# Row-maximum scores as two 512-column matmuls in a fused window-attention and linear-attention kernel

## The reference

```python
# layer 0: per window of S=64 tokens, C=128 channels, 8 heads of dh=16
normed = layernorm(win, ln1_g, ln1_b)
q, k, v = split(normed @ in_w.T + in_b)
scores = einsum('bhsd,bhtd->bhst', q, k) / sqrt(16)
attn = softmax(scores)
win = win + einsum('bhst,bhtd->bhsd', attn, v) @ out_w.T + out_b
h = layernorm(y, ln2_g, ln2_b)
y = y + silu(h @ fc1_w.T + fc1_b) @ fc2_w.T + fc2_b
# layer 1: per image, N = 1024 positions, E = 64
q, k, v = wq x + bq, wk x + bk, wv x + bv
out = wo ((q k^T / N) v) + bo + x
```

## Time and profile before

| | us |
|---|---|
| median of 3 runs (377.37 to 381.28) | 377.72 |
| profiled execution, its own time | 377.23 |
| its span, first to last instruction | 375.4 |
| PE busy in it | 349.0 (93%) |
| DVE busy | 294.3 (78%) |
| ACT busy | 241.7 (64%) |
| scores for the maxima, PE L611, 512 matmuls | 54.4 |

### The profile page before, as it was taken

One profiled execution on the slowest core, in us unless ns is written; L12 is line 12 of the kernel. 1 busy time (PEld: TensorE's weight loads), 2 busy tenths in 40 slices (PEclk: granted clock), 3 DMA queues, 4 the chain that ended last, 5 costly groups with the idle time before them and its releaser, 6 DMA issues.

```text
span 375.4 us, 9822 instructions
## 1 busy us (share of the span) xinstructions
PE 349.0 (93%) x3349; PEld 294.9 (79%) x3349; DVE 294.3 (78%) x863; ACT 241.7 (64%) x438; POOL 167.2 (45%) x176
## 2 busy tenths in 40 slices
PE   3679999999999999999999999999999999999764
PEld 2567788888888888888888888888888888878552
DVE  8387889798788878898788878898798878687452
ACT  1426677774969478784969478684969478664540
POOL 6353054644455434645455434635455434431420
PEclk9999999999999999999999999999999999999898
DMA  4133140403122121403122121403122120300101
GB/s 126 34 88 81 33 109 9 113 2 82 60 77 63 41 70 56 111 1 77 63 76 64 38 74 56 109 3 77 63 72 68 35 77 31 86 2 18 40 1 56
DMA packets 31570, 21.94 MB, mean 58 GB/s; under 512 B 22272, under 2 KB 23360, under 8 KB 31552
## 3 DMA queue, kind: packets, MB, share of 16 engines
q1 hardware_dynamic: 31552, 21.71, 21.1%
HBM read 4.92 MB, written 4.19 MB: 24 GB/s over the span
## 4 chain that ended last, share of the span: by engine, by line
PE 76%; DVE 6%; issue 4%; ACT 2%; POOL 1%; DVEq 0%; POOLq 0%; ACTq 0%
PE p_scoreT L634 12%; PE p_c L529 11%; PE p_score L611 9%; PE p_attn L649 9%; PE p_a L529 6%; PE p_scoreT L629 4%; PE p_a L593 4%; PE p_c L707 3%; PE p_d L529 3%; DVE xn_tok L1105 3%; PE p_c L678 2%; PE p_d L719 2%; PE p_a L577 2%; PE p_a L567 2%; PE p_c L684 2%
## 5 line engine op out<-in xcount | busy, mean ns | idle before, releaser
L910 ACT ACTIVATE probs<-p_scoreT 128x512 f32<-128x512 f32 x64 | 38.6, 603 | 35.1 <-PE p_scoreT L634 34.6
L465 POOL TENSOR_TENSOR hid_l<-hid,hid_h 128x512 fp32r<-128x512 f32 x30 | 40.3, 1364 | 43.5 <-ACT hid_h L944 41.6
L611 PE MATMUL p_score<-kd_h,qd_h 128*128 128x128 f32 (+1 forms) x512 | 54.4, 249 | 0.9 <-DVE row_max L1158 0.8
L611 PEld LDWEIGHTS p_score<-kd_h,qd_h 128*128 128x128 f32 (+1 forms) x512 | 50.0, 163 | 5.9 <-DVE row_max L1158 2.4
L649 PEld LDWEIGHTS p_attn<-vd,probs 128*64 128x64 f32 x1024 | 36.2, 139 | 22.2 <-issue 15.1
L470 POOL TENSOR_TENSOR y_l<-y,y_h 128x512 fp32r<-128x512 f32 (+1 forms) x17 | 20.5, 1208 | 69.4 <-ACT y_h L924 69.4
L1158 DVE TENSOR_REDUCE row_max<-p_score 128x8 f32<-128x512 f32 x64 | 43.9, 687 | 6.7 <-PE p_score L611 6.7
L649 PE MATMUL p_attn<-vd,probs 128*64 128x34 f32 x1024 | 45.7, 245 | 2.7 <-ACT probs L910 2.7
L457 POOL TENSOR_SCALAR kd_l<-k_l,head_a 128x512 fp32r<-128x512 f32 x16 | 26.7, 1669 | 33.5 <-DVE k_l L1140 19.8
L634 PE MATMUL p_scoreT<-qd_h,kd_h 128*128 128x256 f32 x128 | 41.3, 322 | 0.0
L449 POOL TENSOR_TENSOR rstd<-rstd,minus_half 128x4 f32<-128x4 f32 (+1 forms) x33 | 35.5, 1076 | 2.8
(11 more groups left out here) (183 smaller groups left out, 877.9 us busy)
## 6 DMA issues: line engine op xcount, KB each, us to landing
x_in<-in_x SPq DMA_DIRECT2D x16, 256.0 KB, 2.9
qd_h<-q_h SPq DMA_DIRECT2D x64, 64.0 KB, 2.0
qd_l<-q_l SPq DMA_DIRECT2D x64, 64.0 KB, 2.0
vd<-v_tok SPq DMA_DIRECT2D x64, 64.0 KB, 2.2
out<-out_sb SPq DMA_DIRECT2D x16, 256.0 KB, 2.1
fc_rows<-in_L_conv_fc_w SPq DMA_DIRECT2D x2, 128.0 KB, 2.5
in_w_rows<-in_L_conv_in_w SPq DMA_DIRECT2D x1, 192.0 KB, 2.7
out_w_rows<-in_L_conv_out_w SPq DMA_DIRECT2D x1, 64.0 KB, 2.4
```

The lines of the kernel that those rows point to most:

```text
L465: pool.tensor_tensor(hid_l[:, t], hid[:, t], hid_h[:, t].bitcast(F32), ALU.subtract).then_inc(hid_low[t], 1)
L611: last = pe.matmul(p_score[0:rows, 2 * KEYS * j:2 * KEYS * (j + 1)], qd_h[:, h.par, j, 2 * KEYS * p:2 * KEYS * p + rows], kd_h[:, h.par, 2 ...
L910: act.activation(probs[:, p % 2], p_scoreT[:].rearrange("row (win j q) -> row win j q", win=2, j=QUADS), ACT.Exp, scale=SCORE_SCALE).then_ ...
```

## The change

It has two parts.

1. **Scores for the maxima.** Now the keys are spread instead of q: a new tile `km_h`, zero outside its blocks, holds for each head pair j the keys of all windows in that pair's 32 rows only. The weights are `q_h` of the pair's 128 (64) queries, the moving operand is `km_h[:, par, :, window]`, four blocks of 128 columns: one matmul of 512 columns per window, two per pair of windows. `km_h` is filled from `kd_h` by four DMAs of 128 KB (`spread_k`), once both `kd_h` blocks are there. `q_h` has two parities now. The first score of a step waits for `km_dma`; the wait for `qd_h` and `kd_h` goes to `b_scoreT`. GpSimd zeroes both parities of `km_h` (4096 elements per partition each) in the prologue, and sets `vd` later.
2. **Order.** On TensorE `a_q` goes ahead of the tail's `c_fc2`, and `a_k` takes the place behind `c_yT`. On ScalarE `a_xn` goes behind `c_o` at the end of the step before, `a_q`, `a_k` and the first `a_k_block` ahead of `b_exp(1)`, the second right behind it. On VectorE `a_xn` goes ahead of `c_y1`, `a_q` ahead of `c_y2`, `a_k` ahead of `c_kv`.

```diff
-        q_h = sb("q_h", [C, HALF], F32R)
+        q_h = sb("q_h", [C, 2, HALF], F32R)
+        km_h = sb("km_h", [C, 2, QUADS, 2 * HALF], F32R)
...
+            def spread_k(h):
+
+                sp.wait_ge(kd_high[0], h.n())
+                sp.wait_ge(kd_high[1], h.n())
+                if h.follows(2):
+                    sp.wait_ge(score_ready[PAIRS - 1], h.n(2))
+                for j in range(QUADS):
+                    head_pair = slice(32 * j, 32 * j + 32)
+                    sp.dma_start(km_h[head_pair, h.par, j, :].bitcast(F32),
+                                 kd_h[head_pair, h.par].rearrange("p win a k -> p (win a k)").bitcast(F32)
+                                 ).then_inc(km_dma, 16)
...
             def prologue(loop):
                 sp.wait_ge(q_zero_set[0], 2)
                 spread_q(loop.half(0))
+                sp.wait_ge(km_zero_set[0], 1)
+                spread_k(loop.half(0))
                 sp.wait_ge(v_const_set, 5)
                 spread_v(loop.half(0))
...
                 rstd1_of(loop.half(0))
+                set_values()
                 pool.memset(qd_h[:, 1].bitcast(F32), 0.0).then_inc(q_zero_set[1], 1)
                 pool.memset(qd_l[:, 1].bitcast(F32), 0.0).then_inc(q_zero_set[1], 1)
+                pool.memset(km_h[:, 1].bitcast(F32), 0.0).then_inc(km_zero_set[1], 1)
                 k_low_block(loop.half(0))
...
             def b_score(h, p):
 
                 if p == 0:
-                    pe.wait_ge(q_high_dma, h.n(times=16 * QUADS))
-                    pe.wait_ge(kd_high[0], h.n())
-                    pe.wait_ge(kd_high[1], h.n())
+                    pe.wait_ge(q_high, h.n())
+                    pe.wait_ge(km_dma, h.n(times=16 * QUADS))
...
-                for j in range(QUADS):
-
-                    for win, rows in ((1, 2 * KEYS), (0, KEYS)):
-                        last = pe.matmul(p_score[0:rows, 2 * KEYS * j:2 * KEYS * (j + 1)],
-                                         qd_h[:, h.par, j, 2 * KEYS * p:2 * KEYS * p + rows],
-                                         kd_h[:, h.par, 2 * p + win], start=True, stop=True)
+                for win, rows in ((1, 2 * KEYS), (0, KEYS)):
+                    window = 2 * p + win
+                    last = pe.matmul(p_score[0:rows, :], q_h[:, h.par, 2 * KEYS * p:2 * KEYS * p + rows],
+                                     km_h[:, h.par, :, 2 * KEYS * window:2 * KEYS * (window + 1)], start=True, stop=True)
...
                 b_score(b, 2)
+                if with_a:
+                    a_q(a)
                 if with_tail:
                     c_fc2(tail)
                 b_attn(b, 0)
                 if with_c:
                     c_yT(c)
                 if with_a:
-                    a_q(a)
+                    a_k(a)
                 if with_tail:
                     c_kv(tail)
                 b_scoreT(b, 1)
                 b_score(b, 3)
                 if with_d:
                     d_kvT(loop, -1)
-                if with_a:
-                    a_k(a)
                 b_attn(b, 1)
```

More of the change, by code:

```diff
@@ L352, in spread_q @@
                     head_pair = slice(32 * j, 32 * j + 32)
-                    sp.dma_start(qd_h[head_pair, h.par, j, :].bitcast(F32), q_h[head_pair, :].bitcast(F32)
+                    sp.dma_start(qd_h[head_pair, h.par, j, :].bitcast(F32), q_h[head_pair, h.par, :].bitcast(F32)
                                  ).then_inc(q_high_dma, 16)
@@ L389, in step_even @@
                 spread_q(loop.half(1))
+                spread_k(loop.half(1))
                 spread_v(loop.half(1))
@@ L395, in step_odd @@
                     spread_q(loop.half(2))
+                    spread_k(loop.half(2))
                     spread_v(loop.half(2))
@@ L416, in _, with set_values @@
             pool.memset(minus_half[:], -0.5).then_inc(const_ready, 1)
-            pool.memset(vd[:], 0.0).then_inc(v_const_set, 1)
-            pool.wait_ge(v_const_set, 1)
-            for a in range(2):
-                for s in range(2):
-                    pool.memset(vd[64 * a:64 * a + 64, s, :, a, DH, :], 1.0).then_inc(v_const_set, 1)
-            pool.wait_ge(v_const_set, 5)
+            pool.memset(km_h[:, 0].bitcast(F32), 0.0).then_inc(km_zero_set[0], 1)
+            def set_values():
+                pool.memset(vd[:], 0.0).then_inc(v_const_set, 1)
+                pool.wait_ge(v_const_set, 1)
+                for a in range(2):
+                    for s in range(2):
+                        pool.memset(vd[64 * a:64 * a + 64, s, :, a, DH, :], 1.0).then_inc(v_const_set, 1)
+                pool.wait_ge(v_const_set, 5)
             def waited():
@@ L619, in b_scoreT @@
                 if p == 0:
+                    pe.wait_ge(q_high_dma, h.n(times=16 * QUADS))
                     pe.wait_ge(q_low_dma, h.n(times=16 * QUADS))
+                    pe.wait_ge(kd_high[0], h.n())
+                    pe.wait_ge(kd_high[1], h.n())
                     pe.wait_ge(kd_low[0], h.n())
@@ L876, in a_q @@
                 act.wait_ge(q_ready, h.n())
-                if h.follows(1):
-                    act.wait_ge(q_high_dma, h.n(1, times=16 * QUADS))
-                act.activation(q_h[:], p_a[0][:], ACT.Identity, bias=qkv_b[:, 0:1]).then_inc(q_high, 1)
+                if h.follows(2):
+                    act.wait_ge(q_high_dma, h.n(2, times=16 * QUADS))
+                if h.follows(2):
+                    act.wait_ge(score_ready[PAIRS - 1], h.n(2))
+                act.activation(q_h[:, h.par], p_a[0][:], ACT.Identity, bias=qkv_b[:, 0:1]).then_inc(q_high, 1)
             def a_k(h):
@@ L892, in a_k_block @@
                     act.wait_ge(scoreT_ready[PAIRS - 1], h.n(2))
+                if h.follows(2):
+                    act.wait_ge(km_dma, h.n(2, times=16 * QUADS))
                 act.wait_ge(k_high, h.n())
@@ L970, in prologue @@
                 a_v(a)
+                a_xn(loop.half(1))
             def step(loop, b, with_a, with_next, with_c, with_tail, with_d, with_last=False):
@@ L981, in step @@
                 if with_a:
-                    a_q(a)
+                    a_k(a)
+                    a_k_block(a, 0)
                 b_exp(b, 1)
                 if with_a:
-                    a_k(a)
-                    a_k_block(a, 0)
+                    a_k_block(a, 1)
                     a_v(a)
@@ L1003, in step @@
                     c_o(b)
+                if with_next:
+                    a_xn(next_a)
                 if with_d and not with_last:
@@ L1130, in a_q @@
                     dve.wait_ge(q_low_dma, h.n(1, times=16 * QUADS))
-                dve.scalar_tensor_tensor(q_l[:], p_a[0][:], qkv_b[:, 0:1], q_h[:].bitcast(F32),
+                dve.scalar_tensor_tensor(q_l[:], p_a[0][:], qkv_b[:, 0:1], q_h[:, h.par].bitcast(F32),
                                          ALU.add, ALU.subtract).then_inc(q_low, 1)
@@ L1293, in step @@
                 b_widen(b, 1)
+                if with_a:
+                    a_xn(a)
                 if with_c:
```

15 lines of the change are left out of this document (6 added, 9 removed).

## The result

| | before | after |
|---|---|---|
| median of 4 runs each, us | 377.55 (377.09 to 381.28) | 386.64 (385.47 to 389.18) |
| profiled execution, its own time, us | 377.23 | 389.18 |
| its span, us | 375.4 | 387.3 |
| TensorE busy, us | 349.0 (93%) | 346.0 (89%) |
| first score of step 0, us | 20.50 | 24.89 |

The account below looks back on a forecast made before the run. TensorE looked bound, but the new order would make VectorE bound the first half of a step. Terms 4.1 + 0.5 - 0.2 + 7 x 0.1 + 6 x 0.4 - 0.4 = +7.1 us on 377.23: 384.3, median 384.5, range 373.5 to 390.

Parts of the forecast that it names:

- first score: Prologue: the first score waits for the keys' DMAs, starting at 24.6 instead of 20.50; +4.1 us (3.8 to 4.7).
- step 0: First step: the second keys' DMAs land 17.6 us behind the first score, the step lasting 16.6; +0.5 us.
- step 1: Second step, with no tail and few pieces on VectorE; -0.2 us.
- seven even steps: Steps 2 to 14: the scores' savings vanish as TensorE waits for `xn_l` before q; +0.1 us each.
- six odd steps: Odd steps: `q_l` and `k_l` delay `kv_tok` on VectorE, so `d_kvT` starts 1.4 us later; +0.4 us each.
- step 15 and the rest: Last step, which has no stage a; -0.4 us.
- the 0.5 to 0.8 given as the sign: Before q in each step: TensorE would wait 0.5 to 0.8 us on `xn_l`.
- TensorE stays the bound: Rival: VectorE keeps up, so each of 14 steps saves 0.8 us; 370.2 us, chance 0.13.
- Half of it survives: Rival: waits in front of q shorten later ones, so 14 steps save 0.4 us each; 375.8 us, chance 0.2.
- Worse: Rival: no wait shortens another, even steps +0.3 us, odd +0.8; 388 us, chance 0.15.
- The keys are late in every step: Rival: SyncE's groups or landings take 2 us more, even steps +1 us; 391 us, chance 0.02.
- the signs given: Included even steps of 18.9 to 19.1 us, odd ones of 23.6 to 24.1, and the clock at full speed.

Follow-up runs that it names:

- experiment 1: Changed kernel plus 19 unread matmuls of 512 columns on TensorE, filling the wait before the first scores; 386.49 us, ratio 1.018 to the kernel before.
- experiment 3: Changed kernel's new order, but old scores in all steps and no spreading of keys; 383.41 us, ratio 1.011 to the kernel before.
- experiment 8: Changed kernel with the edits of experiment 2 and experiment 7, `c_kv` behind the fourth scores, q behind attention 0 where no tail; 376.25 us, ratio 0.993.
- experiment 9: As experiment 8, but `c_kv` moved behind the fourth scores in even steps alone; 371.54 us, ratio 0.982 to the kernel before.
- experiment 7: Changed kernel with the moves of experiment 5 (TensorE) and experiment 6 (VectorE) together; 379.36 us, ratio 1.002 to the kernel before.
- experiment 6: Changed kernel with two moves on VectorE: `y2` ahead of `q_l`, `kv_tok` ahead of `k_l`; 385.64 us, ratio 1.019 to the kernel before.
- experiment 4: Changed kernel's new scores, but the old order on TensorE, ScalarE and VectorE; 400.44 us, ratio 1.057 to the kernel before.
- experiment 5: Changed kernel with one move on TensorE: q behind the tail's `c_fc2`; 392.88 us, ratio 1.036 to the kernel before.
- experiment 2: Changed kernel, but step 0 takes the old scores and its keys are spread behind v; 381.45 us, ratio 1.007 to the kernel before.
- experiment 10: Order of experiment 9 with old scores in all steps and no key DMAs; 377.24 us, ratio 0.998 to the kernel before.

## Why the prediction came out right, and where it did not

The sign held, and so did the waits that were named. Most of the loss lies elsewhere than in the order, though: 9.3 of the 11.9 us are the first score and step 0, where the prediction had 4.6 of 7.1. The terms, against the profiled execution:

| term | predicted | measured | difference |
|---|---|---|---|
| first score | +4.1 | +4.39 | +0.3 |
| step 0 | +0.5 | +4.87 | **+4.4** |
| step 1 | -0.2 | +0.05 | +0.2 |
| seven even steps | +0.7 | +2.42 | +1.7 |
| six odd steps | +2.4 | +0.37 | -2.0 |
| step 15 and the rest | -0.4 | -0.15 | +0.2 |
| sum | +7.1 | +11.9 | +4.8 |

**The first score.** Read rightly from the earlier trace rows: the keys were issued from 20.56 (20.43 predicted) and landed in 2.4 us (2.3 taken). GpSimd's new memsets ended at 17.37 and `kd_l` was begun 0.17 later, at the same time as before: nothing, by little, as said.

**Step 0 is the term that was mis-sized, +0.5 for +4.87.** The prediction asked only whether the second set of keys would be late at its end, and took the clock to stay full. The 4.6 us of idle TensorE at the start, which it had itself worked out, were followed by a fall of the granted clock, and step 0 ran at half speed for most of its length: experiment 1 puts that at 2.1 to 3.0 us of the profiled step. The rest is open between the remaining clock loss and the order: q goes forward to a place where `xn_l` is not ready, and waits 1.33 us, and experiment 3, with no keys at all, has 18.70 for step 0, some of it clock.

The reason given for +0.5 was nevertheless a sound one. It reckoned 17.6 us from the first score to the landing of the second keys. In after's slowed step they kept nobody waiting. At the full clock they do: they land 17.8 us behind the first score in experiments 8 and 9, and end step 0 there. The half microsecond by which q's DMAs are earlier is 0.2 to 0.4 (8.0 us behind the first score in experiment 1 and 8.2 in experiment 3, against 8.4).

**Even steps: VectorE does bound the first half, and one cover was missed.** `xn_l` was ready at 4.77 and q started at 4.92 (5.02 predicted for both), and `c_fc2` ended at 7.2 as predicted. TensorE's wait before q was 0.41, and 0.30 in the odd step, less than the 0.5 to 0.8 given as the sign. The savings of the first two pairs were lost sooner than thought: `b_scoreT(0)`, behind them, starts at 2.34 in the changed kernel and at 2.41 in the one before, since it waits for the widened maxima; the prediction had counted 0.49 there and lost it only at q, so its total up to there was right for a partly wrong reason. The miss of a quarter microsecond a step lies further on. The prediction let the fourth pair save 0.16 and added 0.1 for ScalarE's queue; but from that pair to attention 1 it now takes 0.85, because k no longer stands there to cover the exponential. The cause that it expected, `q_h` and `kd_h` ahead of `b_exp(1)`, is not it: the exponential starts at 204.45 as soon as `b_scoreT(1)` is done, 0.22 of ScalarE's own idle time ahead of it. Experiments 7 and 8 bear it out: with `c_kv` in the gap an even step goes from 18.73 to 18.47.

**Odd steps: the right wait, about half its size, and a sixth of its cost.** `d_kvT` waits for `kv_tok`, which ended 12.36 into the step (12.9 predicted, 10.59 before). The last score ends at 12.0 as predicted, so the wait is 0.5 us where 0.85 was reckoned, and the step grows by 0.07 where 0.4 was. The prediction took 0.4 of `q_l`'s 1.3 us of idle time to replace waits that VectorE had. `q_l` did wait 1.36 us, but `kv_tok` came 1.77 later than before, 0.37 more than the 1.4 counted for the two added pieces, so 1.0 of the idle time was absorbed. Attention 1 ends at 14.07 (14.02 before). Experiment 6 removes the wait and the odd step loses 0.35 us.

**The rivals.** "TensorE stays the bound" (370.2) was wrong for this order, and is what experiment 9 reaches with another one: 371.5. Its condition was put rightly, that the results of VectorE come in time. "Half of it survives" (375.8) asked that waits in front of q shorten others behind; nothing of the saving was left at the end of a step. "Worse" (388) lies nearer to the median than the forecast does, 1.4 us against 2.1. It had +0.3 for an even step, which is about what it came to (0.35 on average), but +0.8 for an odd one, which cost 0.07, so it is near for the wrong steps. "The keys are late in every step" needs the old order (experiment 4), where it costs far more than the 391 worked out.

**The sum.** The median lies 2.1 us above the forecast, with errors of +4.4, +1.7 and -2.0 in the profiled execution: the even and odd steps nearly cancel, and the median holds less of the clock's loss than the profiled execution, which lies 4.9 above its 384.3. (384.3 and the half microsecond between profile and median make 384.8, not 384.5.) Of the signs given, even steps (19.21), odd steps (23.51) and the clock all fell outside what was said. That the number came out so near is in good part luck.

## What to carry to other kernels

When a change saves time on the engine that looks bound, count what the moved or shortened piece was covering: k between a score and an attention sum covered an exponential, and without it TensorE idles 0.38 us there, where the shorter score had saved 0.17. An engine held by its neighbour's results may need both orders changed together: here one half alone did harm (from 1.023 to 1.036), the other gave little (1.019), and both gave 1.002. And the added wait of 4.6 us on TensorE was paid twice in the profiled execution, once for itself and once, 2 to 3 us, for the clock behind it; at the full clock the next thing in line, the second keys' DMAs, cost 0.7.

## What was not expected of the hardware

- After 4.6 us without work on TensorE the granted clock was 0.50 for 10 us and 0.54 for 5 more, although the engine was busy 86% of them. In experiment 4, with the same first wait, it was 0.50 from 24.9 to 30 and 1.00 from 30 to 35. Experiments 5 and 6 are as after, and 7 lies between (0.81 from 30 to 35). What sets the length was not settled.
- In runs of the same first instructions the clock reached its full level for the first time at 15.7 to 18.9 us, which moved the first score by up to 1.1 us (20.17 in experiment 2, 21.29 in 3).
- The clock also fell in part in step 0 of kernels with no such wait: 0.81 and 0.85 from 20 to 30 in experiment 2, 0.89 and 0.77 from 24.9 to 35 in experiment 3. In experiments 8 to 10 it stayed at 1.00 there.
- A DMA of 32 partitions with 128 KB landed in 2.4 us; four take SyncE 2.42 us to issue, and four of 64 KB took 2.49, so twice the bytes did not lengthen the issuing of these.
